# Attention of a hybrid block in units of four heads: float32 scores from 32-row strips instead of float32r stacks in pairs

## What is computed

```python
x = x + scan_block(group_norm(x))             # projections, 3x3 conv, 4 selective scans, gate
t = t + attn(ln(t), causal)                    # layer 0: 12 heads of 16
t = t + ffn_block(ln(t))                       # layer 1: full attention, MLP, then 4 experts, top 2
# attn:
qkv = x @ W_attn + b_attn
scores = einsum('bqhd,bkhd->bhqk', q, k) / sqrt(16)   # layer 0 masked above the diagonal
out = einsum('bhqk,bkhd->bqhd', softmax(scores), v) @ W_proj + b_proj
```

## Time and profile before

| | |
|---|---|
| median of 3 executions | 899.87 us (895.37 to 905.07) |
| the profiled execution | 906.1 us; its span from first to last instruction 904.1 us |
| mean granted TensorE clock in it | 0.826 of full |
| blocks start at (us of the span) | 0, 143.8, 326.9, 516.8, 704.5, 834.1 |

### The profile page before, as it was taken

The page is one execution under the profiler, slowest core; times in us unless marked ns, Lnnn a source line. Parts: engine busy times, 40 slices in busy tenths (PEclk is TensorE's granted clock), DMA queues, the critical chain, the costliest instruction groups (busy, mean ns, idle before and its releaser), DMA issues. The chain is left out here.

```text
span 904.1 us, 8598 instructions
## 1 busy us (share of the span) xinstructions
PE 634.5 (70%) x3104; PEld 422.4 (47%) x3104; DVE 570.0 (63%) x931; ACT 306.4 (34%) x571; POOL 215.5 (24%) x184
## 2 busy tenths in 40 slices
PE   1405556583557768885878788967888878887597
PEld 1201114342322347464534565655446656765486
DVE  3559964666689845775699658675998444533210
ACT  0133303122323204256254232555443234343131
POOL 5215540131234410103244201022343110000100
PEclk9999656575678759787899888888889898999789
DMA  6988810035567100048274000364660000000000
GB/s 151 285 189 197 194 39 9 1 36 130 124 139 180 30 9 1 9 65 209 67 178 115 14 5 0 46 169 108 152 162 9 0 1 1 1 1 9 1 1 9
DMA packets 28623, 68.87 MB, mean 76 GB/s; under 512 B 5152, under 2 KB 12976, under 8 KB 28592
## 3 DMA queue, kind: packets, MB, share of 16 engines
q1 hardware_dynamic: 28592, 68.47, 32.6%
HBM read 60.33 MB, written 3.93 MB: 71 GB/s over the span
## 5 line engine op out<-in xcount | busy, mean ns | idle before, releaser
L1536 POOL TENSOR_TENSOR state<-state,C_rows 128x1024 f32<-128x1024 f32 x42 | 113.3, 2697 | 203.1 <-DVE state L1112 203.1
L1112 DVE TENSOR_TENSOR_SCAN state<-decay,dx_rows 128x512 f32<-128x512 f32 x84 | 127.6, 1559 | 12.7 <-PE py L679 8.9
L679 PE MATMUL py<-state,sel 128*96 128x512 f32 x168 | 100.2, 735 | 46.7 <-POOL state L1536 46.6
L1401 ACT ACTIVATE decay<-d_rows,a_neg 128x255 f32<-128x255 f32 x192 | 81.4, 496 | 132.1 <-DMA d_rows<-delta_dram 96.1
L750 PE MATMUL pd<-w_dn,act 128*128 128x192 f32 x480 | 90.5, 343 | 3.7 <-ACT act L1414 3.7
L1105 DVE TENSOR_TENSOR dx_rows<-dx_rows,B_rows 128x1024 f32<-128x1024 f32 x48 | 74.4, 1551 | 21.4 <-DMA dx_rows<-delta_x_dram 21.4
L750 PEld LDWEIGHTS pd<-w_dn,act 128*128 128x128 f32 x480 | 82.7, 200 | 7.1 <-ACT act L1414 4.6
L679 PEld LDWEIGHTS py<-state,sel 128*96 128x96 f32 x168 | 30.8, 197 | 94.7 <-POOL state L1536 57.8
L734 PE MATMUL pu<-fT,w_up 128*128 128x256 f32 x180 | 61.6, 426 | 12.1 <-ACT act L1414 11.7
L532 PE MATMUL ps<-hT,w_qkv 96*96 96x256 f32 x128 | 44.1, 519 | 33.9 <-DVE hT L1255 33.2
L905 PE MATMUL pm<-probs,v_aug 128*32 128x256 f32 (+1 forms) x384 | 52.2, 397 | 13.8 <-DVE inv_den L1314 8.2
(11 more groups left out here) (230 smaller groups left out, 1151.8 us busy)
## 6 DMA issues: line engine op xcount, KB each, us to landing
d_rows<-delta_dram SPq DMA_DIRECT2D x48, 512.0 KB, 6.6
dx_rows<-delta_x_dram SPq DMA_DIRECT2D x48, 512.0 KB, 5.2
w_dn<-exp_w_dram SPq DMA_DIRECT2D x1, 2304.0 KB
B_rows<-xdbl SPq DMA_DIRECT2D x4, 512.0 KB, 7.0
C_rows<-xdbl SPq DMA_DIRECT2D x4, 512.0 KB, 10.8
w_up<-exp_w_dram SPq DMA_DIRECT2D x1, 1536.0 KB
delta_dram<-delta SPq DMA_DIRECT2D x4, 384.0 KB, 3.0
delta_x_dram<-delta_x SPq DMA_DIRECT2D x4, 384.0 KB, 3.4
```

The lines of the kernel that those rows point to most:

```text
L679: mm = nc.tensor.matmul(py[0:INNER, :], sel[:, first:first + INNER], flat(states[g % held])[:, paths], start=False, stop=(g == GROUPS - 1) ...
L1112: ins = nc.vector.tensor_tensor_scan(flat(states[g % held])[:, both], flat(decay[g % 2])[:, both], dx_rows[g % 2][:, both], 0.0, ALU.mult, ...
L1401: ins = nc.scalar.activation(decay[g % 2][:, k, rest], d_rows[g % 2][:, k, rest], ACT.Exp, scale=a_neg[:, at:at + 1])
L1536: nc.gpsimd.tensor_tensor(now, now, C_rows[:, :], ALU.mult).then_inc(sc_done, 1)
```

## The change

The high and low parts, the stacks and their float32r tiles go. Host code lays the query and key weights out so that the projection itself gives each head 32 rows, 16 filled and 16 zero: six outputs of 128 channels (12 float32 products, 24 instructions) instead of four of 96 (8 products, 16 instructions). ACT copies the queries with bias (3 instructions), DVE the keys with bias (3); the row of ones comes in with the keys' bias, added once. A unit is now four heads in 32-row strips of the array, one PSUM bank a head, in float32 (two instructions a product). There are three units, all four banks of `ps` belong to one unit, and probs is one buffer of the size of the two before. So scores(u+1) wait for the exponentials of unit u, and row_max(u+1) is issued after spread(u). The twelve slots stay, four to a unit. The weights loaded once grow from 432 KB a layer (`w_qkv`) to 720 KB (`w_qk` 576, `w_v` 144), with two loads more in all. POOL's constants in the first block lose 12 selections and two copies and gain two selections.

```diff
-                        for c in range(2):
-                            for part in range(2):
-                                first = WIDTH * part + CGROUP * c
-                                chunks(ps[0:CGROUP, 2 * c + part, 0:TOKENS],
-                                       lambda ch: w_qkv[l][:, ch, first:first + CGROUP],
-                                       lambda ch: hT[:, ch, :]).then_inc(qk_done[l], 1)
+                        for part, ht in ((0, 0), (0, 1), (1, 0), (1, 1), (0, 2), (1, 2)):
+                            chunks(ps[:, part + 2 * (ht // 2), TOKENS * (ht % 2):TOKENS * (ht % 2 + 1)],
+                                   lambda ch: w_qk[l][:, ch, part, ht, :],
+                                   lambda ch: hT[:, ch, :]).then_inc(qk_done[l], 1)
...
-                        for u in range(4):
-                            stack(u)
                         others((l, "projected"))
-                        for u in (4, 5):
-                            stack(u)
...
                         def scores(u):
                             if u == 0:
+                                pe.wait_ge(q_copied[l], HTILES)
+                                pe.wait_ge(k_copied[l], HTILES)
+                            else:
+                                pe.wait_ge(p_done[l], u)
+                            for i in range(TILES):
+                                keys = 128 * (i + 1) if causal else TOKENS
+                                for j in range(QUAD):
+                                    rows = slice(32 * j, 32 * j + HEAD)
+                                    mm = nc.tensor.matmul(ps[:, j, TOKENS * i:TOKENS * i + keys],
+                                                          q_quad[rows, u, 128 * i:128 * (i + 1)],
+                                                          k_quad[rows, u, 0:keys],
                                                           start=(i == 0), stop=not causal,
+                                                          tile_position=(32 * j, 0), skip_group_check=True)
...
+                            for kt in range(TILES):
+                                q0 = 128 * kt if causal else 0
+                                for j in range(QUAD):
+                                    row = slice(32 * j, 32 * j + 32)
+                                    mm = nc.tensor.matmul(pm[row, q0:TOKENS], v_aug[:, kt, QUAD * u + j, :],
+                                                          probs[:, j, kt, q0:TOKENS],
...
                         scores(0)
-                        for u in range(UNITS):
-                            if u + 1 < UNITS:
+                        for u in range(HTILES):
+                            row_max(u)
+                            others((l, 4 * u))
+                            shifted(u)
+                            others((l, 4 * u + 1))
+                            if u + 1 < HTILES:
                                 scores(u + 1)
-                            row_max(u)
-                            if u >= 1:
-                                context(u - 1)
-                            others((l, 2 * u))
-                            shifted(u)
-                            if u in (2, 4):
-                                spread(u // 2 - 1)
-                            others((l, 2 * u + 1))
-                        context(UNITS - 1)
+                            others((l, 4 * u + 2))
+                            context(u)
+                            others((l, 4 * u + 3))
+                            if u + 1 < HTILES:
+                                spread(u)
```

On DVE, `row_max(0)` and then for each of the three units:

```diff
+                            shift(u)
+                            others((l, 4 * u))
+                            others((l, 4 * u + 1))
+                            if u + 1 < HTILES:
+                                row_max(u + 1)
+                            others((l, 4 * u + 2))
+                            if u + 1 < HTILES:
+                                context_copy(u)
+                            others((l, 4 * u + 3))
+                            if u + 1 < HTILES:
+                                invert_sums(u)
```

More of the change, by code:

```diff
@@ L35 @@
 CGROUP = WIDTH // 2
[L37 to L39 removed]
+TOP_ROW = HEAD
 CH = [(0, 128), (128, 64)]
@@ L44 @@
 A_LOG_MAX = 80.0
-SLOTS = [(l, s) for l in range(2) for s in ("turned", "projected", *range(2 * UNITS), "context", "spread",
+SLOTS = [(l, s) for l in range(2) for s in ("turned", "projected", *range(HEADS), "context", "spread",
                                             "output")]
@@ L230, in build @@
         hT = sb("hT", [CGROUP, 2, TOKENS])
[L232 to L237, removed]
+        q_quad = sb("q_quad", [128, HTILES, TOKENS])
+        k_quad = sb("k_quad", [128, HTILES, TOKENS])
         v_aug = sb("v_aug", [128, TILES, HEADS, 32])
-        top = sb("top", [128, 2, TILES, 128], F32R)
-        probs = [sb(f"probs{i}", [128, 2, 2, TOKENS]) for i in range(2)]
+        top = sb("top", [128, TILES, 128])
+        probs = sb("probs", [128, QUAD, TILES, TOKENS])
         inv_den = sb("inv_den", [128, TOKENS])
@@ L503, in attention_constants @@
                                          pattern=[[-32, QUAD], [0, 32]], channel_multiplier=1))
-            for j in range(2):
+            for j in range(QUAD):
                 link(nc.gpsimd.affine_select(
                     out=top_one[:, :], in_=top_one[:, :], compare_op=ALU.not_equal, fill=1.0,
-                    base=-(64 * j + TOP_ROW), pattern=[[0, 1]], channel_multiplier=1))
-            spread_of = cT[:, 0:2, :].rearrange("p a (x j r i) -> p a x j r i", x=2, j=2, r=4)
-            for part in range(2):
[L510 to L517, removed]
+                    base=-(32 * j + TOP_ROW), pattern=[[0, 1]], channel_multiplier=1))
             link(nc.gpsimd.tensor_copy(identb[:, :], ident[:, :]))
@@ L557, in block_of @@
             if opening:
-                states += [buf[:, :, :, :].rearrange("p j t q -> p (j t) q") for buf in probs]
+                states += [probs[:, 2 * b:2 * b + 2, :, :].rearrange("p j t q -> p (j t) q") for b in range(2)]
             held = len(states)
@@ L814, in attention @@
                                         lambda c: hT[:, c, 128 * tl:128 * (tl + 1)],
[L815 removed]
+                                        lambda c: w_v[l][:, c, :])
                         mm.then_inc(v_done[l], 1)
[L818 to L822, removed]
[L823 to L830 removed]
@@ L884, in shifted @@
                                                           start=(i == 0), stop=not causal,
[L885 removed]
+                                                          tile_position=(32 * j, 0), skip_group_check=True)
                             if causal:
[L887 to L892 removed]
+                                mm = masks(maskk)
@@ L1350, in _ @@
                         dve.wait_ge(w_b, 16 * len(b_loads))
+                    if split_w_up:
+                        for l in range(2):
+                            link(nc.vector.tensor_scalar(b_qk[l][:, 1, :], b_qk[l][:, 1, :], top_one[:, :], None,
+                                                         ALU.add))
                     if run_a:
@@ L1662 @@
     }
+    for l in range(2):
+        host[f"w_qk{l}"] = heads_apart(w_qkv[l][:, 0:2 * WIDTH]).reshape(2, CGROUP, 2, HTILES, 128) \
+            .transpose(1, 0, 2, 3, 4)
+        host[f"b_qk{l}"] = heads_apart(b_qkv[l][0:2 * WIDTH])[0].transpose(2, 0, 1)
+        host[f"w_v{l}"], host[f"b_v{l}"] = w_qkv[l][:, 2 * WIDTH:], b_qkv[l][2 * WIDTH:]
     nc = bacc.Bacc("TRN2", target_bir_lowering=False, num_devices=1)
```

203 lines of the change are left out of this document (70 added, 133 removed).

## The result

The change made the kernel slower: 928.62 us (921.93 to 940.7), before 900.88; ratio 1.0287, 95% interval 1.0169 to 1.0405. Run again with the experiments it took 926.64, ratio 1.0261 (1.0201 to 1.0321). Forecast were 892 and a range of 876 to 908.

The account below looks back on a forecast made before the run. No engine was full throughout: PE and DVE alternate with scans, PE's chain binds without. Block terms (+0.5; -1.2 - 1.5; twice -2.5 + 3.0; -6.5; 0) sum to -7.7 us, taking the median 899.87 to 892; range 876 to 908.

Parts of the forecast that it names:

- The strips side by side: Scores of four heads: four float32 strips run at once, 0.75 us a causal set, 0.95 a full one.
- Rival D: Scores: strips don't run side by side, each set costs 1.9 or 2.5 us more; 970 us; chance 0.07 in both forms.
- its milder form: Scores: products start in order of issue, nine steps instead of four in a full set; 922 us; shares the 0.07 chance.
- PE's work: All eight layers: PE loses net 3 to 4.5 us of work a layer.
- DVE's and ACT's work: Each layer: DVE loses about 5 us; ACT's exponential about 1.9 us against twice 1.02, its copies from ten to three.
- Full layers with scans: Second to fourth block: 3.0 us longer in the third and fourth, 1.5 us shorter in the second.
- rival A: Scan layers: DVE's saved time counts after all, 2.4 us less each; 876 us; chance 0.19.
- Stacks against projection: Layer start: stacks go, about 2 us; the projection grows by 8 instructions, 1.7 to 3.5 us.
- the walk through the causal layers: Engine orders followed through a causal layer: gain 7 us in the fifth block, 1.2 in the second, 2.5 in third and fourth.
- The full layer without scans: Fifth block: PE idle about 1.7 us five times, the layer ending 0.5 us later.
- Rival C: Unit hand-overs cool PE's clock, 2.6 us more in each of eight layers; 913 us; chance 0.10.
- a granted clock under 0.79: PE's clock over the run: forecast near 0.82; under 0.79 would show that hand-overs cool the clock.

Follow-up runs that it names:

- the repeat: A second profile of the changed kernel with nothing altered; 924.9 us of span.
- experiment 3: Changed kernel with the turned maximum and shift of unit u+1 moved ahead of the spread and reciprocal of unit u; 911.20 us, ratio 1.0060.
- 1 with 3: Changed kernel with scores and shifted scores reading all 32 rows of a strip, and turn and shift ahead of spread and reciprocal; 894.59 us, ratio 0.9900.
- experiment 1: Changed kernel with scores and shifted scores reading all 32 rows of a strip instead of 16 and 17; 917.68 us, ratio 1.0144.

## Why the prediction was wrong, point by point

**The strips side by side** held: 0.87 and 1.08 us a set for my 0.75 and 0.95, 48 sets, 6 us of PE more than I had. Rival D and its milder form, in which products start in program order, are out: a full set would have taken nine steps of 0.21 us and some 2.0 us in all; its sixteen instructions start in four groups of four, the last 0.75 us behind the first. (That the two halves of a float32 product are issued one behind the other, no row shows.) D's 970 leaves out the 7.7 us gained; with them it would be 963. The Trainium skill, "TensorE: Matmul & The Clock Gate", section The mechanism, has that order; the trace disagrees again, and its 922 us lies near the measured time by luck.

**PE's work** fell by 29 to 32 us at full clock, as forecast (24 to 36), though the range of 3 to 4.5 us a layer is that of the causal layers: the same sum gives 2 to 3.8 for a full one.

**DVE's and ACT's work** held. Groups of DVE and ACT, after, to be held against the earlier trace rows:

```profile
L1234 DVE TENSOR_REDUCE top<-ps 128x8 f32<-128x2048 f32 x12 | 27.4, 2280 | 20.5 <-PE ps L814 20.5
L1253 DVE RECIPROCAL inv_den<-pm 128x256 f32<-128x256 f32 x24 | 41.9, 1747 | 13.3 <-PE pm L867 13.1
```
```profile
L1413 ACT ACTIVATE probs<-ps 128x2048 f32<-128x2048 f32 x12 | 22.5, 1876 | 57.6 <-PE ps L838 57.6
```

**Full layers with scans**, +3.0 each and -1.5 in the second block, held: +3.0, +2.3 and -2.4, and for the reason given: the sum is read 6.4 us behind the last scan in f2 and f3 for my 6.5, and 4.6 before. So rival A is out: DVE's saved time brought nothing there.

**Stacks against projection.** I had the first scores of the fifth block 8.4 us behind the projection's start (708.1 to 716.5). They came after 11.0 us (11.2 in the repeat, clock 0.71), and after 8.0 in the profiles where that stretch was at 2.4 GHz (3, and 1 with 3, among others). My 1.7 to 3.5 us for the wider projection was right at full clock, and I used its lower part for a layer start that I had myself called half-clocked.

**The step that failed** is the walk through the causal layers, "Gain 7 us" and -1.2, -2.5, -2.5. It took every duration at 2.4 GHz and priced an idle place at its own length. In c4 its times can be held against the runs, in us behind the projection's start:

| | walk | repeat | 3 |
|---|---|---|---|
| first scores | 8.4 | 11.2 | 8.0 |
| turn(0) | 11.6 | 14.6 | 11.4 |
| shifted(0) | 15.9 | 18.8 | 15.7 |
| end of `down` | 21.2 | 24.3 | 21.1 |
| shifted(1) | 28.5 | 31.5 | 26.4 |
| shifted(2) | 40.2 | 45.7 | 38.8 |
| bias | 44.2 | 51.1 | 43.5 |

Where PE had 2.4 GHz, the walk is right within 0.4 us up to the end of `down` (from there on experiment 3 has another order). In the repeat 2.8 us are lost to half clock before the first scores and another 4 from shifted(1) on, where a causal set takes 1.67 us again; 6.9 us of the 7 are gone. The idle places were in the walk ("PE idle 2.5 and 1.8 us", and that between the first scores and the turn, 716.5 and 719.7, unnamed); what they do to the clock was not. In c2 and c3 the idle place behind the first scores was followed by up to 13.6 us at half clock, and cost 6 us of layer.

A second part is the order. In c4 the walk's times hold the shift behind copy, spread and reciprocal. For the second to fourth block it gave a gain from an earlier last reciprocal and no price for the shift, though the next pair's shift stood ahead of them before; even at clock 0.78 c2 took 97.8 us for the 95.9 forecast. Moving it brought 15 us in all (experiment 3), part of them by the clock.

**The full layer without scans**, +0.5, came out at +6.7 and +3.4. The walk had PE idle five times for 1.7 us; it idles six times for 0.9 to 2.6, 10.2 us in all, in both profiles, and at half clock behind some of them. PE's timeline of f4 in the repeat:

```profile
812.19 0.70 PE L711 MATMUL pu<-fT,w_up 128*128 128x256 f32 x2 [2.62 <-ACT act L1359]
...
814.24 2.09 PE L814 MATMUL ps<-k_quad,q_quad 16*128 16x256 f32 x16
```

Behind the wait the next set takes 2.09 us in place of 1.15.

**Rival C** was the right mechanism, at 0.10 and 913 us, and its sign, a granted clock under 0.79, was there (0.776 and 0.788). Its price was half a stretch, 2.6 us, in each of eight layers. Measured, it costs 6 us where it strikes in c2 and c3, where PE is on the path, and half clock in a projection another 3; the full layers with scans (0.69 to 0.90) came out as forecast without a price for it, as I had argued. And part of it, 9 us by experiment 1, had a cause that no row of the kernel before shows: strips of 16 and 17 rows. Between the kernels lie 22 us in the runs of the experiments (926.6 and 904.6); 1 and 3 together take 32 off. How the 15 us of experiment 3 divide into a shorter chain and a warmer PE stays open, but for the 3.2 us ahead of c4's first scores, which are clock.

## What to carry to other kernels

When a change takes away double buffering, look first for the place where the other buffer's work used to run while an engine waited, and price it by the stretch at half clock that follows it, not by its own length; a loop that runs twice in one profile may show both prices. Issue what the next unit needs ahead of what only this unit's tail needs (here the shift ahead of spread and reciprocal), and check what stands ahead of each half of such a pair in its own queue. In strips, read all 32 rows where the rest holds zeros: it costs no time, and at 32 rows the clock rose where at 17 it stayed down.

## What the runs showed of the hardware that I had not expected

- The granted clock depends on more than PE's busy time: over one list of products, without a break, it stayed at 1.2 GHz for 11.2 us with 16 and 17 rows a strip (four profiles) and rose to 2.4 within 6.0 us with 32 (six profiles). Ratios with the early shift: 1.0060, 0.9959 and 0.9900 for 17, 24 and 32 rows, the middle one weak.
- Two turns of one loop, with the same instructions and the same idle place of 1.9 us, differed by 9.1 us (97.8 and 106.9) by the clock alone: 2.9 us ahead of that place and 6.0 behind it. It fell behind the place only in layers whose first scores had come late.
- The highest mean clock (0.835 to 0.859) did not go with the lowest time: 896.18 us, against 889.45 at 0.826 to 0.847.
